# A causal attention layer with eight pairs of heads: another order of its rows of queries, and four sets of probability buffers

## What is computed

```python
def _L0_attn_a_ref(x, W_K, W_Q, W_V, W_O):
    K = jnp.einsum('bpd,ihd->biph', x, W_K)
    Q = jnp.einsum('bpd,ihd->biph', x, W_Q)
    V = jnp.einsum('bpd,ihd->biph', x, W_V)
    scores = jnp.einsum('biph,biqh->biqp', K, Q)
    mask = jnp.tril(jnp.ones((q_len, q_len), dtype=bool))
    scores = jnp.where(mask[None, None, :, :], scores, NEG_INF)
    attn = jax.nn.softmax(scores / np.sqrt(d_head).astype(np.float32), axis=-1)
    z = jnp.einsum('biph,biqp->biqh', V, attn)
    z_flat = jnp.transpose(z, (0, 2, 1, 3)).reshape(b, q_len, -1)
    return jnp.einsum('bqf,df->bqd', z_flat, W_O)

x = x + attn_a(layernorm(x));  x = x + experts(layernorm(x), w1, b1, w2, b2)
x = x + attn_b(layernorm(x));  x = x + experts(layernorm(x), w1, b1, w2, b2)
```

## Time and profile before

| | |
|---|---|
| median of three runs | 1334.13 us (1332.97 to 1335.38) |
| the profiled execution | 1330.41 us, of which the span from the first to the last instruction is 1328.7 us |
| busy in the span | PE 1176.7 us (89%), DVE 932.4 (70%), POOL 838.5 (63%), ACT 792.0 (60%) |
| weight loads of PE (PEld) | 864.7 us (65%) |
| first projection, last addition of attention | 20.01 us, 1016.91 us |
| DMA | 55.64 MB, mean 42 GB/s |

### The profile page before, as it was taken

The page is one execution under the profiler, slowest core; times in us unless marked ns, Lnnn a source line. Parts: engine busy times, 40 slices in busy tenths (PEclk is TensorE's granted clock), DMA queues, the critical chain, the costliest instruction groups (busy, mean ns, idle before and its releaser), DMA issues. The chain is left out here.

```text
span 1328.7 us, 24368 instructions
## 1 busy us (share of the span) xinstructions
PE 1176.7 (89%) x8058; PEld 864.7 (65%) x8058; DVE 932.4 (70%) x2059; ACT 792.0 (60%) x2189; POOL 838.5 (63%) x797
## 2 busy tenths in 40 slices
PE   6999999999999999999999999999996394898485
PEld 4676677676766776776767676767764394455385
DVE  5887678868786777688677867777873454577554
ACT  5777577757666675777576766757762053232143
POOL 1676658757875776677578757766774453554444
PEclk9899999999999999999999999999998597899588
DMA  4600700170034007001600350020000121000023
GB/s 126 175 2 13 140 1 1 33 124 1 1 87 66 2 1 144 13 1 33 121 1 1 76 81 1 1 64 1 1 1 9 41 64 52 1 1 1 31 63 96
DMA packets 74451, 55.64 MB, mean 42 GB/s; under 512 B 7925, under 2 KB 63225, under 8 KB 74329
## 3 DMA queue, kind: packets, MB, share of 16 engines
q1 hardware_dynamic: 71832, 48.96, 17.8%
q0 software_dynamic: 2496, 5.13, 1.2%
HBM read 13.29 MB, written 24.01 MB: 28 GB/s over the span
## 5 line engine op out<-in xcount | busy, mean ns | idle before, releaser
L325 POOL TENSOR_SCALAR at_prob<-at_prob,at_scale 128x512 f32<-128x512 f32 (+1 forms) x480 | 656.2, 1383 | 5.6
L353 DVE TENSOR_REDUCE at_nmax<-at_ps 128x1 f32<-128x512 f32 (+3 forms) x640 | 375.7, 603 | 153.8 <-PE at_ps L519 149.9
L434 ACT ACTIVATE at_prob<-at_ps,at_nmax 128x512 f32<-128x512 f32 (+3 forms) x640 | 393.2, 623 | 44.4 <-DVE at_nmax L353 43.6
L530 PE MATMUL at_ps<-ident,at_prob 128*128 128x128 f32 x2176 | 328.8, 275 | 23.4 <-DVE at_probT L376 19.1
L530 PEld LDWEIGHTS at_ps<-ident,at_prob 128*128 128x128 f32 x2176 | 255.8, 140 | 110.7 <-issue 52.7
L448 ACT ACTIVATE at_probT<-at_ps 128x512 f32<-128x512 f32 (+1 forms) x288 | 165.1, 573 | 212.6 <-PE at_ps L530 188.0
L516 PE MATMUL at_ps<-at_k_st,at_q_parts 128*128 128x512 f32 (+3 forms) x640 | 285.1, 446 | 6.2 <-ACT at_prob L434 3.7
L545 PE MATMUL at_ps<-at_probT,at_v 128*64 128x256 f32 (+1 forms) x2304 | 270.1, 374 | 12.0 <-DVE at_probT L376 11.9
L519 PE MATMUL at_ps<-at_k_st,at_q_parts 128*128 128x512 f32 (+3 forms) x640 | 253.5, 397 | 0.0
L376 DVE COPY at_probT<-at_ps 128x512 f32<-128x512 f32 (+1 forms) x288 | 188.9, 656 | 68.2 <-PE at_ps L530 65.0
L545 PEld LDWEIGHTS at_ps<-at_probT,at_v 128*64 128x64 f32 x2304 | 155.3, 136 | 106.6 <-issue 48.1
(11 more groups left out here) (197 smaller groups left out, 1304.1 us busy)
## 6 DMA issues: line engine op xcount, KB each, us to landing
at_q_parts<-at_q_parts SPq DMA_DIRECT2D x64, 256.0 KB, 3.6
slots_in<-zeros SPq DMA_DIRECT2D x6, 1483.5 KB, 16.4
slots_in<-zeros SPq DMA_DIRECT2D x6, 1419.0 KB, 15.6
f_xs<-slots_in SPq DMA_DIRECT2D x46, 64.5 KB, 1.8
wall<-in_L_ffn_w_dram SPq DMA_DIRECT2D x1, 2048.0 KB, 10.8
wall<-in_L_ffn_w_dram SPq DMA_DIRECT2D x4, 512.0 KB, 6.4
f_got<-slots_out SPq DMA_DIRECT2D x8, 256.0 KB, 3.5
out_dram<-x SPq DMA_DIRECT2D x4, 256.0 KB, 2.3
```

What stands on the lines that cost most here:

```text
L325: pool.tensor_scalar(cols, cols, scale[:, k, u, c:c + 1], None, ALU.mult).then_inc(s_fix["pool"], 1)
L353: dve.tensor_reduce(nmax[:, j % 2, u % 4, c:c + 1], bank, AX.X, ALU.max, negate=True).then_inc(s_max, 1)
L434: act.activation(prob[j % 2][u % 4][:, c * BANK:c * BANK + w], ring[use_of["score", p, u, c] % RING][:, 0:w], ACT.Exp, bias=nmax[:, j % 2, ...
L530: last = pe.transpose(turn_ps[h][:, b * P:(b + 1) * P], prob[j % 2][2 * i + h][:, t * P:(t + 1) * P], ident[:, :])
```

## The change

ROW_ORDER takes the rows as 4, 3, 5, 2, 6, 1, 7, 0, so that a long one and a short one stand in turn; everything that counted rows by STEPS * p + j now goes by their place in this order, and the maxima, sums and scales of a row by the place's parity. ROW_HOME gives each row one of four sets of probability buffers; an exponential waits for the last turn of the row that had the same set before (row_before), which is always four places back. A scale on GpSimd waits in addition for DVE's last fix two places back. The chunks are projected in the order 0, 2, 1, 3; in the plan a projection waits for the last score that reads the chunk it overwrites (last_reader), a value projection for the last product with it (last_value). A score waits for the keys of its own chunk, and a row's first one for its queries. In the plan a score costs at least 0.2 us, and the tie-break by name is gone. Normalised x, the turned weights and the first set of probability buffers lie in one piece of memory ("late"), which the experts' weights take over: they are loaded behind the last pair's projections and the last turn of row 6 (load_wall), at the end of SyncE's queue in attention. No instruction that computes is added or left out.

```diff
+ROW_ORDER = (4, 3, 5, 2, 6, 1, 7, 0)
+ROW_HOME = (2, 3, 2, 3, 0, 1, 0, 1)
+CHUNK_ORDER = (0, 2, 1, 3)
...
+    everything = [(p, j) for p in range(PAIRS) for j in ROW_ORDER]
+    place = {pj: q for q, pj in enumerate(everything)}
+    groups = [(p, j, g) for p, j in everything for g in range(j + 1)]
+    group = {pjg: n for n, pjg in enumerate(groups)}
...
+    def score_steps(j):
+        return [(i, h, c) for i in range(2) for h in range(2) for c in range(chunks(j))]
...
+    def row_before(q):
+
+        return next((everything[b] for b in range(q - 1, -1, -1) if ROW_HOME[everything[b][1]] == ROW_HOME[everything[q][1]]), None)
+
+    def last_reader(c, i):
+
+        j = [j for j in ROW_ORDER if (chunks(j) > c if i == 0 else 2 * j // TPC == c)][-1]
+        return (j,) + [s for s in score_steps(j) if i == 1 or s[2] == c][-1]
+
+    def last_value(m):
+        j = [j for j in ROW_ORDER if chunks(j) > m][-1]
+        return j, run_of(j, min(2 * m + 1, j))[-1]
...
     for p in range(PAIRS):
-        last_score = p and ("pe", "score", p - 1, ROWS - 1, NC - 1)
-        for c in range(NC):
+        for c in CHUNK_ORDER:
             for kind in range(2):
-                step(("project", p, c, kind), "pe", 0.87, last_score)
+                step(("project", p, c, kind), "pe", 0.87, p and ("pe", "score", p - 1) + last_reader(c, kind))
...
-            step(("vproject", p, c), "pe", 0.47, p and last_value(STEPS * p - 1))
+            step(("vproject", p, c), "pe", 0.47, p and ("pe", "value", p - 1) + last_value(c))
...
-        n = chunks(j)
-        for u in range(4 * j, 4 * j + 4):
-            for c in range(n):
-                w = width(u, c) / BANK
-                step(("score", p, u, c), "pe", 0.43 * w + 0.2 * (c == n - 1), ("sp", "second", p, row(u) // TPC))
-                step(("max", p, u, c), "dve", 0.15 + 0.54 * w, ("pe", "score", p, u, c), q > 1 and ("pool", "scale") + everything[q - 2])
-                step(("exp", p, u, c), "act", 0.42 + 0.42 * w, ("dve", "max", p, u, c),
-                     q > 1 and ("pe", "turn") + everything[q - 2] + (1, (j - 2) % STEPS))
-        last = ("act", "exp", p, 4 * j + 3, n - 1)
+        n, old = chunks(j), row_before(q)
+        for i, h, c in score_steps(j):
+            w = width(j, i, c) / BANK
+            step(("score", p, j, i, h, c), "pe", max(0.43 * w, 0.2) + 0.2 * (c == n - 1),
+                 ("dve", "low", p, c, 0), ("sp", "second", p, 2 * j // TPC))
+            step(("max", p, j, i, h, c), "dve", 0.15 + 0.54 * w, ("pe", "score", p, j, i, h, c), q > 1 and ("pool", "scale") + everything[q - 2])
+            step(("exp", p, j, i, h, c), "act", 0.42 + 0.46 * w, ("dve", "max", p, j, i, h, c), old and ("pe", "turn") + old + (1, old[1]))
+        last = ("act", "exp", p, j) + score_steps(j)[-1]
...
-        xnT = sb("xnT", [D, T])
-        wT = {n: sb("wT_" + n, [P, PAIRS, P]) for n in "qkv"}
+
+        late, at = keep["late"], 0
+
+        def early(cols):
+            nonlocal at
+            at += cols
+            return late[:, at - cols:at]
+
+        xnT = early(T)
+        wT = {n: early(PAIRS * P).rearrange("p (a f) -> p a f", f=P) for n in "qkv"}
...
-        prob = [[sb(f"prob{k}{i}", [P, T - P * (i < 2) - 2 * P * (k == 0)]) for i in range(4)] for k in range(2)]
+        prob = []
+        for k in range(max(ROW_HOME) + 1):
+            longest = max(j for j in range(STEPS) if ROW_HOME[j] == k)
+            cols = [(2 * longest + 1 + u // 2) * P for u in range(4)]
+            prob.append([early(n) if k == 0 else sb(f"prob{k}{u}", [P, n]) for u, n in enumerate(cols)])
...
-                    if c == NC - 1:
+                    if c == CHUNK_ORDER[-1]:
                         fetch(sp, p)
+                sp.wait_ge(s_proj, 2 * NC * PAIRS)
+                sp.wait_ge(s_vproj, NC * PAIRS)
+                j = [j for j in ROW_ORDER if ROW_HOME[j] == 0][-1]
+                for h in range(2):
+                    sp.wait_ge(s_turn[h], group[PAIRS - 1, j, j] + 1)
+                keep["load_wall"](sp)
...
                     elif kind == "scale":
                         pool.wait_ge(s_rinv, q + 1)
+                        if q >= 2:
+                            p2, j2 = everything[q - 2]
+                            pool.wait_ge(s_fix["dve"], count_of["dve", "fix", p2, j2, chunks(j2) - 1, 1, 1])
...
+                        _, _, j, i, h, c = it
+                        q = place[p, j]
+                        if (i, h, c) == (0, 0, 0) and q >= 2:
                             dve.wait_ge(s_scale, q - 1)
...
-                        if c == 0 and STEPS * p + j >= 2:
-                            act.wait_ge(s_turn[h], group(*divmod(STEPS * p + j - 1, STEPS), 0))
-                        act.wait_ge(s_max, count_of["dve", "max", p, u, c])
...
+                        if (i, c) == (0, 0) and old:
+                            act.wait_ge(s_turn[h], group[old + (old[1],)] + 1)
+                        act.wait_ge(s_max, count_of["dve", "max", p, j, i, h, c])
...
-                        if r % TPC == 0 and u % 4 == 0 and c == 0:
-                            pe.wait_ge(s_lo, count_of["dve", "low", p, r // TPC, 1])
-                            pe.wait_ge(s_second[r // TPC], 32 * (p + 1))
+                        _, _, j, i, h, c = it
+                        r, w = 2 * j + i, width(j, i, c)
+                        if (i, h) == (0, 0):
+                            pe.wait_ge(s_lo, count_of["dve", "low", p, c, 0])
+                            if c == 0:
+                                pe.wait_ge(s_lo, count_of["dve", "low", p, r // TPC, 1])
+                                pe.wait_ge(s_second[r // TPC], 32 * (p + 1))
...
                 sp.dma_start(rows[:, a:b, :], keep["zeros"][:, :].unsqueeze(1).to_broadcast([P, b - a, D + 1])).then_inc(keep["s_scratch"], 16)
-        if p:
-            return
+
+    def load_wall(sp):
...
-            "wall": sb("wall", [P, E, 2 * hid + shp.FCH + D]),
+            "late": sb("late", [P, shp.T + 3 * shp.PAIRS * P + 2 * (2 * NT - 5) * P]),
...
+        row = 2 * hid + shp.FCH + D
+        keep["wall"] = keep["late"][:, 0:E * row].rearrange("p (e n) -> p e n", n=row)
```

More of the change, by code:

```diff
@@ L116, in attention_plan @@
                 for i in range(2):
-                    w = width(4 * j + 2 * i + h, c) / BANK
-                    length = {"pool": 0.28 + 1.28 * w, "dve": 0.1 + 0.5 * w, "act": 0.2 + 0.45 * w}[fixer(h, i)]
-                    step(("fix", p, j, c, h, i), fixer(h, i), length, ("pool", "scale", p, j), last)
-    groups = [(p, j, g) for p, j in everything for g in range(j + 1)]
+                    w = width(j, i, c) / BANK
+                    length = {"pool": 0.28 + 1.28 * w, "dve": 0.1 + 0.5 * w}[fixer(h, i)]
+                    step(("fix", p, j, c, h, i), fixer(h, i), length, ("pool", "scale", p, j))
     for q, (p, j) in enumerate(everything):
@@ L187, in attention_plan @@
         running = [(t, s) for t, s in running if t > now]
-    return order, row, chunks, width, turned, fixer, run_of
+    return order, everything, place, group, row_before, chunks, width, score_steps, turned, fixer, run_of
 def attention(nc, shp, keep, x_in, w_k, w_q, w_v, w_o, fetch):
@@ L196, in attention @@
     STEPS = NT // 2
-    order, row, chunks, width, turned, fixer, run_of = attention_plan(PAIRS, NT, NC, TPC)
+    order, everything, place, group, row_before, chunks, width, score_steps, turned, fixer, run_of = attention_plan(PAIRS, NT, NC, TPC)
     uses = [it for it in order["pe"] if it[0] in ("score", "project", "vproject", "out")]
@@ L550, in _ @@
                         j = it[2]
-                        q = STEPS * p + j
+                        q = place[p, j]
                         free_bank(it)
```

96 lines of the change are left out of this document (42 added, 54 removed).

## The result

The changed kernel takes 1291.53 us (median of four runs, 1289.25 to 1294.6) against 1333.55 us of the kernel before on the same chip (1332.14 to 1335.38): a ratio of 0.9685, interval 0.9668 to 0.9701. It is 42 us faster.

A forecast was written before the change was run, and what follows sets the result against it. The prediction took PE to bound the kernel and summed changes in its idle time: -16.5 - 4.3 - 1 + 6 + 2.5 = -13.3 from 1330.41, thus 1317.1. With the median 3.7 us higher it forecast 1321 us, range 1304 to 1352.

The forecast's parts named there:

- Order and four sets: Pairs of heads: PE idle time falls from 4.45 to 1.7 us a pair, 16.5 us less over six, 4.3 in the last.
- Switches on PE: Scores beside turns take 0.55 us, behind scores 0.47; 1 us less taken, bounds 6 us more and 6 us less.
- The change of pairs: Between pairs: first score about 14.5 us after the first projection, PE covered for 13.5 of it, 0.9 us idle left.
- The start: First pair: later first score and turn, 4.5 us more idle, taken as 6 us slower; bounds 2 and 15 us.
- The 1.5 us for the clock: First pair: a lower granted clock during thin supply raises the start's cost from 4.5 to 6 us.
- The tail: Row 7's last fixes to attention's last addition: 2.5 us more; bounds 2 us less and 6 us more.
- The weights' load: Experts' weights loaded late, SyncE done some 9 us early: costs nothing, up to 5 us if it reaches the barrier.
- GpSimd's new wait: Scales waiting for DVE's last fix two rows back: 0 to 0.5 us a pair, taken as 0.
- tight packing: Rival, 1304 us, chance 0.17: all gaps of the pairs closed (-33), switches -6, start and tail 8.5 us.
- The change doesn't do what it says: Rival, 1343 us, chance 0.20: sets and order only move the gaps, start and tail cost 8.5 us on top.
- The change of pairs starves PE: Rival, 1355 us, chance 0.18: too little turned work at each change of pairs, 6.2 us idle against 4.45.

The follow-up runs named there:

- e3: The changed kernel with its planner told that exponentials wait for the row two places back, as if for two sets: 1491.61 us.
- e5: The changed kernel with rows 3, 5, 7, 1, 2, 6, 4, 0 and chunks 1, 0, 3, 2, four sets with their own homes: 1282.66 us.
- after: The changed kernel itself, against the kernel before the change: 1291.53 us, ratio 0.9685.
- e4: The changed kernel with the chunks projected in order 0, 1, 2, 3: 1304.7 us.
- before: The kernel before the change, timed on the same chip as the changed kernel: 1333.55 us.
- e2: The changed kernel with rows in the old order 0 to 7, chunks in order and three sets of buffers: 1336.88 us.
- e1: The changed kernel with rows in the old order 0 to 7, chunks in order and two sets of buffers: 1348.58 us.
- e11: e5 with the planner's old lengths for a score and an exponential, as in the kernel before: 1289.3 us.
- e10: e1 with projections released whole in the plan, by the last score and value product of the pair before: 1323.54 us.
- e14: e13 with the unused bank given to the turns of head 1, every engine's order held: 1317.79 us.
- e16: e15 with the unused bank given to the turns of head 1, every engine's order held: 1504.92 us.
- e8: The kernel before with only the late load of the experts' weights: 1331.07 us, ratio 1.0008.
- e9: The changed kernel, every engine's order kept, with exponentials waiting for the row three places back: 1287.94 us.
- e7: The changed kernel with the planner's old lengths for a score and an exponential: 1285.85 us.
- e13: The kernel before with a score ring of four banks instead of five, planned for it, the fifth left unused: 1333.66 us.
- e15: e3 with a score ring of four banks instead of five, planned for it, the fifth left unused: 1530.33 us.

## Why the prediction was wrong

The direction and the cause named were right, the sum was not. The step that failed most is its very basis, that it can be made in PE's idle time: busy time, for which the term for switches allowed a gain of 1 us, fell by 14.0. The gain in idle time and the start were mis-sized too. Term by term:

*Order and four sets: -20.8 forecast, -29.6 measured* (24.4 in six pairs, 5.2 in the last). Mechanism right, size off, within its bound of 33. The step that failed is how I split the 4.45 us of a pair: by place, keeping 0.8 us late in the pair and 0.9 at its change. By cause, 22.6 of the 26.7 us were waits for evictions, wherever they stood, and what puts a score between two turns takes away all of them; 0.38 us a pair is left. I had read one such gap and had written down its reason, but never asked for the list of waits of the six pairs, which gives it with its share.

*Switches on PE: -1 forecast, -14.0 measured* (9.5 in six pairs and 4.5 in the last), outside its bound of 6. This is the largest miss. I priced how a score's time depends on its neighbours (0.08 us each) and never priced a turn's. A turn of four that stands before a score holds PE for 0.36 us (226 such before, 237 after); one that stands before another turn holds it for 0.56 us of "busy" and 0.22 idle in e3 (162 of them). Over the kernels the turns' sum grows with their number: TT of 5, 13, 24, 58, 90 and 93 (e5, after, e4, before, e2, e1) go with 161.6, 160.2, 160.6, 171.3, 177.0 and 178.3 us. e3 has 210 and at full clock 34.0 us in a pair, 204 in six: (204 - 160.2) / (210 - 13) = 0.22 us each, and the 45 fewer from before to after are 10 us of the 11.1 that the turns lost. The number isn't all of it: e11 has 15 with 166.9 us, e10 has 85 with 172.1. Besides the turns' 11.1 us, outputs lost 2.2 and scores 1.2, and projections took 4.5 us more. e14 and e16 show the cause of it, the bank, by holding the order; that all of the 14.0 us are of this kind is an inference from the sums.

*The change of pairs: right in kind.* In the pair that starts at 357.95 row 7's fixes begin at 357.72, 0.2 us ahead of it (forecast 1 to 3 us after, had 8.6), row 0's scale stands 6.9 us behind, and the first score comes 15.5 us after the first projection (forecast 14 to 15). Both lie just outside what was forecast. GpSimd in order of time:

```profile
357.72 6.73 POOL L359 TENSOR_SCALAR at_prob<-at_prob,at_scale 128x512 f32<-128x512 f32 x4
...
364.77 1.56 POOL L359 TENSOR_SCALAR at_prob<-at_prob,at_scale 128x512 f32<-128x512 f32 x1
```

PE in order of time:

```profile
357.95 1.12 PE L597 MATMUL at_ps<-late 128*128 128x512 f32 x2
...
373.46 0.47 PE L552 MATMUL at_ps<-at_k_st,at_q_parts 128*128 128x512 f32 x1
```

The cover that I called thin held: no gap at all in the pair of 119.60 us shown above, and in all six pairs one wait of 0.7 us for the copy of query halves. That the release by chunk changes nothing in the new order was right as well (row 0 comes last, and attention_plan writes the same order with either release); in the old order it is a loss of 25 us.

*The start: +6 forecast, -1.4 measured,* below its lower bound of 2. The events came as forecast: first score 34.28 (33.3), first turn 49.20 (48.5), against the earlier trace rows. PE in order of time:

```profile
34.28 0.47 PE L552 MATMUL at_ps<-at_k_st,at_q_parts 128*128 128x512 f32 x1 [2.55 <-DVE at_k_st L443]
...
49.20 0.63 PE L566 MATMUL at_ps<-ident,late 128*128 128x128 f32 x4 [1.83 <-POOL late L359]
```

The stretches of the first pair, up to the first score, to the first turn, and to the end:

```profile
20.17:34.28 14.11, 10.97 (x49) 6.48 (x49) 9.64 (x14) 12.73 (x22) 0.00 (x0) 1.00 0.30 77
34.28:49.20 14.92, 12.50 (x50) 8.30 (x51) 14.02 (x30) 11.19 (x37) 4.16 (x6) 0.89 0.27 70
49.20:122.74 73.54, 73.00 (x532) 54.92 (x533) 56.48 (x115) 53.88 (x152) 60.90 (x58) 1.00 0.00 1
```

Idle up to the first score is 3.1 us, as forecast. From there to the first turn it is 2.4 us where I had counted 5, since PE ran ahead into row 3's scores and didn't keep to the exponentials' pace; behind it 0.5 us instead of 1.7. So 6.1 us, only 0.8 more than before and not 4.5. Busy time fell by 2.2 us; that these are hidden waits again is likely and not shown. The 1.5 us for the clock went too; stretches as in the earlier trace rows:

```profile
30.00:35.00 5.00, 2.45 (x7) 1.07 (x7) 4.82 (x7) 3.56 (x7) 0.00 (x0) 1.00 0.59 143
35.00:40.00 5.00, 5.00 (x21) 3.81 (x21) 4.62 (x9) 3.54 (x13) 0.00 (x0) 0.66 0.66 177
40.00:45.00 5.00, 4.40 (x20) 2.62 (x18) 4.58 (x11) 4.68 (x16) 0.43 (x2) 1.00 0.00 0
```

The granted clock was 0.66 for 5 us, between the levels of 1.2 and 2.4 GHz in the mean, behind 5 us with PE busy for 2.45; then it was full again. In this stretch PE had time to spare, so slower scores filled what would have been idle. The 11 us that I had drawn from the Trainium skill, "TensorE: Matmul & The Clock Gate", Part 1, did not come: the low clock didn't last through the thin supply. The reading that it would was mine.

*The tail: +2.5 forecast, +2.0 measured,* 29.67 us from row 7's first fix to the last addition (30), though I had the addition near 1004 and it came at 974.03. GpSimd in order of time:

```profile
944.83 3.39 POOL L359 TENSOR_SCALAR at_prob<-at_prob,at_scale 128x512 f32<-128x512 f32 x2
...
948.33 16.83 POOL L359 TENSOR_SCALAR at_prob<-at_prob,at_scale 128x512 f32<-128x512 f32 x13
```

*The weights' load: 0, right* (e8). SyncE takes 17.1 us for the ten, from 943.32 to 960.43, and issues nothing more until 976.25. The first reader starts at 1006.9, 32.5 us behind the last addition instead of 26.5. In between DVE stood idle for 5.15 us, up to 1001.40, at a step of the router, for a reason that the profile doesn't show; in e9, e5 and e7, which load as late, the first reader starts 26.4 to 26.5 us behind, so it isn't the loads. What follows attention took 1.7 us more in all, and 309.0 to 315.7 in the runs above, whose code there is the same.

*GpSimd's new wait: 0, right;* POOL is busy for 512.20 us in six pairs, no longer than before, and PE waited 0.4 us for it.

The misses add up: idle -8.8, busy -13.0, start -7.4, tail -0.5, the rest +1.9: -27.9 before rounding, which is -41.2 less the -13.3 of the sum.

Of the rivals, *tight packing* was nearest in kind. Its 0.17 was too low, and even its price was too small: its -6 for the switches was -14.0, for the reason above (I bounded a gain by the idle time shown), and its 8.5 us for start and tail were 0.6. The argument against it, next to no gap left in the 63 us of the earlier trace rows, failed for the same reason. For it I had cited the Trainium skill, "Perfetto Trace Analysis", Identifying the Most-Contended Engine: busy time is a poor measure of headroom. In that the trace agrees, 14 us of "busy" time could be won. But the weight loads' share, 70% before and 73% after (512.04 of 702.99), didn't show how much: e5, with 0.75 us of idle time in six pairs, stands at 73% too. *The change doesn't do what it says* fell with e3 and e1: exponentials wait mostly for maxima and still the depth decides, between two places back (1491.6) and three (1287.9). The list names only the last of an engine's waits. *The change of pairs starves PE* didn't occur.

What the gain belongs to: neither order nor depth has it alone. From e10, the old order with the change's other edits in their best form (1323.5), the new order with three or four places back takes off 35 us; with two places back it adds 170; a third set in the old order takes off nothing. Each of these kernels has its own instruction order from the planner, good for some 6 us (e5 and e11); the pairs e9 with after, e13 with e14 and e15 with e16 have the same order and are free of that.

## What to carry to other kernels

Before pricing a new order, list the waits of the bounding engine over the whole regime by what released them, and price each cause as gone or kept, not each place. Then ask what the idle rows don't show: a matmul row ends later than the next one could start, so the engine's busy time is no lower bound; compare the distance from start to start of the same instruction with different neighbours, and read from that what a neighbour costs. Mixing short and long tiles needs the buffers to let them overlap, and one bank moved from a ring that has too many to a stage that has only one (here 15.9 us) can bring a good third of what a whole reordering does (42 us). Whether the ring has too many is to be measured first: in e3's order the same bank was worth 33 us to the ring.

## What the runs showed of the hardware

PE's busy time for one and the same set of instructions in one and the same order changed by 5.7 us of 712.6 (e13, e14) and by 17.5 of 781.6 (e15, e16, there with a granted clock of 0.97 and 0.98) when only a bank was freed earlier; over all kernels here it went from 698 to 782 us for six pairs. Four transposes in fp32 ahead of a score hold PE for 0.36 us, though their row says 0.60. From the last transpose of head 0's turn to the first of head 1's it takes 0.109 us from start to start with a second bank for head 1 (e14) and 0.224 with one (e13).
